# Last MLP of a vision tower: VectorE takes over the rounding of one hidden chunk in six

## The reference, cut to what matters

```
def _L1_ffn_ref(x0, w1, b1, alpha_w1, alpha_a1, w2, b2, alpha_w2, alpha_a2):
    QN, QP = (-8, 7)
    ...
    xq = _quant_act(x0, alpha_a1)                  # round(clip(x / mean(alpha), -8, 7))
    wq1 = _quant_w(w1, alpha_w1)
    x1 = jnp.einsum('bsd,hd->bsh', xq, wq1)
    x1 = x1 * alpha_w1 * alpha_a1.mean() + b1
    x1 = jax.nn.gelu(x1, approximate=False)
    x1 = jnp.clip(x1, -10.0, 10.0)
    hq = _quant_act(x1, alpha_a2)                  # 768 hidden values a token
    wq2 = _quant_w(w2, alpha_w2)
    x2 = jnp.einsum('bsh,dh->bsd', hq, wq2)
    x2 = x2 * alpha_w2 * alpha_a2.mean() + b2
    return x2
h = h + _L1_ffn_ref(_layernorm(h, axis=-1), ...)
```

## Time and profile before

| | |
|---|---|
| median of 3 runs | 2626.57 us (2626.11 to 2627.27) |
| profiled execution, its own time | 2628.79 us |
| its span | 2627.0 us |
| PE busy | 2499.1 us, 95% of the span |
| DVE busy | 2188.3 us, 83% |
| ACT busy | 2098.1 us, 80% |
| POOL busy | 1079.7 us, 41% |

### The profile page before, as it was taken

The page is one execution under the profiler, slowest core; times in us unless marked ns, Lnnn a source line. Parts: engine busy times, 40 slices in busy tenths (PEclk is TensorE's granted clock), DMA queues, the critical chain, the costliest instruction groups (busy, mean ns, idle before and its releaser), DMA issues. The chain is left out here.

```text
span 2627.0 us, 83621 instructions
## 1 busy us (share of the span) xinstructions
PE 2499.1 (95%) x27865; PEld 2135.4 (81%) x27865; DVE 2188.3 (83%) x5770; ACT 2098.1 (80%) x6210; POOL 1079.7 (41%) x1501
## 2 busy tenths in 40 slices
PE   5899999999998999999999999999999999998786
PEld 5788867888787888888888888888888888886565
DVE  5766668888867888888888888888888888887997
ACT  4777767777756888888888888888888888886998
POOL 5677733333322333333333333333333333342233
PEclk9999999999999999999999999999999999999999
DMA  6334410000003333333333333333333333330111
GB/s 179 105 110 119 117 28 9 0 0 36 9 1 71 74 80 69 73 79 71 73 77 72 73 76 73 73 75 75 73 73 76 73 72 78 73 71 11 46 41 51
DMA packets 181843, 173.27 MB, mean 66 GB/s; under 512 B 19206, under 2 KB 180432, under 8 KB 181520
## 3 DMA queue, kind: packets, MB, share of 16 engines
q1 hardware_dynamic: 181776, 172.44, 27.7%
HBM read 46.49 MB, written 9.68 MB: 21 GB/s over the span
## 5 line engine op out<-in xcount | busy, mean ns | idle before, releaser
L1404 POOL TENSOR_TENSOR b_pr<-b_pr,b_rinv 128x394 f32<-128x394 f32 (+1 forms) x768 | 626.1, 842 | 990.6 <-DVE b_rinv L1362 990.6
L1299 ACT ACTIVATE b_pr<-b_banks,b_nmx 128x197 f32<-128x197 f32 (+1 forms) x1536 | 627.8, 424 | 37.4 <-DVE b_nmx L1356 28.9
L1356 DVE TENSOR_REDUCE b_nmx<-b_banks 128x2 f32<-128x394 f32 (+1 forms) x768 | 395.8, 557 | 63.2 <-PE b_banks L1224 59.4
L1208 PE MATMUL b_banks<-b_xt,wqkv 128*128 128x197 f16 x3840 | 383.1, 249 | 3.7 <-DVE b_qk L1346 2.4
L1208 PEld LDWEIGHTS b_banks<-b_xt,wqkv 128*128 128x128 f16 x3840 | 317.0, 98 | 35.2 <-issue 18.9
L1234 PE MATMUL b_bank_t<-ident,b_pr 128*128 128x128 f32 (+3 forms) x3072 | 333.8, 250 | 2.8 <-DVE b_pt L1327 2.7
L1224 PE MATMUL b_banks<-b_kst,b_qst 128*128 128x197 f16 (+1 forms) x3072 | 327.3, 249 | 1.6 <-ACT b_pr L1299 1.6
L1299 ACT ACTIVATION_READ_ACCUMULATOR b_pr<-b_banks,b_nmx 128x1 f32 (+1 forms) x1536 | 314.2, 205 | 0.0
L1234 PEld LDWEIGHTS b_bank_t<-ident,b_pr 128*128 128x128 f32 (+3 forms) x3072 | 287.7, 141 | 22.5 <-issue 8.4
L1224 PEld LDWEIGHTS b_banks<-b_kst,b_qst 128*128 128x128 f16 (+1 forms) x3072 | 265.4, 105 | 20.9 <-issue 11.0
L1346 DVE SCALAR_TENSOR_TENSOR b_qk<-b_banks,b_qk 128x394 f16<-128x394 f32 x384 | 216.3, 563 | 56.7 <-ACT b_qk L1284 56.7
(11 more groups left out here) (244 smaller groups left out, 4904.7 us busy)
## 6 DMA issues: line engine op xcount, KB each, us to landing
b_qst<-b_qk SPq DMA_DIRECT2D x512, 147.8 KB, 2.6
b_kst<-b_qk SPq DMA_DIRECT2D x512, 73.9 KB, 2.3
patches<-in_x SPq DMA_DIRECT2D x64, 588.0 KB, 4.3
out<-z_res SPq DMA_DIRECT2D x32, 192.0 KB
out<-z_res SPq DMA_DIRECT2D x32, 103.5 KB
m_raw_weights<-in_wqkv SPq DMA_DIRECT2D x2, 1152.0 KB, 6.9
m_raw_weights<-in_w SPq DMA_DIRECT2D x2, 576.0 KB, 5.3
h<-in_fc SPq DMA_DIRECT2D x1, 768.0 KB, 5.9
```

Of the source, the lines that this page charges most:

```text
L1208: last = t.matmul(out[:, g * SEQ:(g + 1) * SEQ], w[:, (2 * n + g) * P:(2 * n + g + 1) * P], x, start=(j == 0), stop=(j == 4))
L1299: last = nc.scalar.activation(pr[n % 3][0:ROWS[c], c, e, :], banks[0:ROWS[c], c, e * SEQ:(e + 1) * SEQ], ACT.Exp, bias=nmx[n % 2][0:ROWS[c ...
L1356: v.reduce_max(nmx[n % 2][0:ROWS[c], c, :], banks[0:ROWS[c], c, 0:2 * SEQ].rearrange("p (e t) -> p e t", e=2), AX.X, negate=True).then_inc ...
L1404: last = nc.gpsimd.tensor_tensor(p, p, inv, ALU.mult)
```

## The change

The sixth chunk (f = 5) of each pair is no longer clipped by DVE and then rounded by ACT. DVE does both in a new function `round_last`, in the other order: it first multiplies by 1/alpha and adds the constant, in place, and then limits the sum to bounds that have been moved into the same whole numbers (`limits`, a tile of 128x2 made once at the start of the stage by two small DVE instructions) while writing `z_hid`. The second instruction waits for the first. ACT rounds the other five chunks. The semaphores follow: `hid_done` and `clipped` count five chunks a pair, `last_done` counts the sixth, PE's `down` waits for both, and gelu 3 waits for `last_done` before it writes the tile that the previous pair's sixth chunk held.

```
-                            (clip_hidden(3, 4, 5), 1), (quantise, 3)])
+                            (clip_hidden(3, 4), 1), (round_last, 1), (quantise, 3)])
...
+                for k, bound in enumerate((S["q_lo"], S["q_hi"])):
+                    last = v.tensor_scalar(limits[:, k:k + 1], bound[:], S["inv_a2"][:, 0:1], ROUND + float(LOW_BITS), ALU.mult, ALU.add)
+                last.then_inc(limits_made, 1)
+                dve.wait_ge(limits_made, 1)
...
+                def round_last(u, b):
+                    a = act_out[(2 * b + LAST) % 4][:]
+                    dve.wait_ge(gelu_made, chunks_before(u, b) + HC)
+                    v.tensor_scalar(a, a, S["inv_a2"][:, 0:1], ROUND + float(LOW_BITS), ALU.mult, ALU.add).then_inc(last_scaled, 1)
+                    dve.wait_ge(last_scaled, 2 * u + b + 1)
+                    dve.wait_ge(made_y[b], u)
+                    v.tensor_scalar(hid[b][:, LAST, :], a, limits[:, 1:2], limits[:, 0:1], ALU.min, ALU.max).then_inc(last_done, 1)
...
                 def round_chunk(u, b, f):
-                    n = chunks_before(u, b) + f
-                    act.wait_ge(clipped, n + 1)
+                    if f == LAST:
+                        return
+                    act.wait_ge(clipped, by_scalar(u, b) + f + 1)
...
                         if not first:
-                            act.wait_ge(hid_done, n - 3)
+                            if f == 3:
+                                act.wait_ge(last_done, 2 * u + b)
+                            else:
+                                act.wait_ge(hid_done, by_scalar(u, b) + f - (3 if f > 3 else 2))
...
                 def down(u, b):
-                    pe.wait_ge(hid_done, chunks_before(u, b) + HC)
+                    pe.wait_ge(hid_done, by_scalar(u, b) + LAST)
+                    pe.wait_ge(last_done, 2 * u + b + 1)
```

More of the change, by code:

```diff
@@ L1431, in mlp_1 @@
             two("made_y"), two("scaled"), two("h_done"), two("stored"))
-        fc_made, gelu_made, clipped, hid_done = map(sem, ("z_fc_made", "z_gelu_made", "z_clipped", "z_hid_done"))
+        fc_made, gelu_made, clipped, hid_done, last_scaled, last_done, limits_made = map(sem, (
+            "z_fc_made", "z_gelu_made", "z_clipped", "z_hid_done", "z_last_scaled", "z_last_done", "z_limits_made"))
+        limits = sb("z_limits", [P, 2])
         scaled_rstd = sem("z_scaled_rstd")
@@ L1441, in chunks_before, with by_scalar @@
             return (2 * u + b) * HC
+        LAST = HC - 1
+        def by_scalar(u, b):
+            return (2 * u + b) * LAST
         LAG = 2
```

## The result

The changed kernel takes 2632.28 us (median of 14 runs) against 2626.72 before (14 runs): ratio 1.0024, 95% interval 1.0017 to 1.0031, so slower by 0.24%. The two medians themselves differ by 5.56 us, 0.21%. The forecast was 2632.5.

What follows compares the result with a forecast made beforehand. It took a ring of 13.55 us for two pairs as the bound, then DVE's own line at 6.98 us a step. Middle 5.4 - 0.2, start 0.7, end 0 make +5.9 us, 2626.57 to 2632.5, range 2628.5 to 2638.

Steps and rivals of the forecast that it cites:

- ring of 13.55 us: Last stage, gelus over clip 5, `quantise`, `finish`, `down`, `up` to gelu: 6.78 us a pair, 13.50 for two after.
- DVE's own line: DVE's step in the last stage without waits: 6.50 us before, 6.98 after the change, then the bound.
- 0.28 us of slack: Room DVE has in each step of the last stage, between its line of 6.50 and the step of 6.78.
- the lower bound: New instructions start 0.08 us before clip 4's end, line 6.96; starting 0.04 after it would make 7.08.
- start, to `finish` 0: Start of the last stage: about 0.25 us for two small instructions and 0.46 from `quantise` behind `round_last`, together +0.7.
- 28 steps in the middle: Middle of the last stage: 27 steps from 6.78 to 6.98 us, +5.4, and -0.2 for the low-clock step.
- from `finish` 28 to 31: End of the last stage: last two pairs without `quantise`, ACT gives back what DVE takes, 0, with 0.5 either way.
- -0.2: The middle step at PE's lower clock was expected at some 8.0 us instead of 8.18.
- ACT's waiting: Last stage: ACT's idle time up by about 0.7 us a pair, part of it in front of rounds.
- B: Rival: the two new DVE instructions cost only 0.28 us more than the old one, 2626 to 2628; chance 0.09.
- C: Rival: ACT is the true pacer, each step loses 0.3 to 0.5 us, 2618 or lower; chance 0.05.
- D: Rival: new DVE instructions take 0.55 us each, 2638, or get caught by POOL's additions, 2648; chance 0.12.

Runs made afterwards that it cites:

- e2: Kernel before, plus one extra DVE clip into an unread tile right in front of the clip of chunk 5: 2633.8 us, ratio 1.0037.
- e3: Kernel before, plus one extra DVE clip into an unread tile in front of the clip of chunk 4: 2629.1 us, ratio 1.0010.
- e4: Kernel before, with the clip of chunk 5 moved behind `quantise` in DVE's order, nothing added or left out: 2620.6 us, ratio 0.9978.
- e8: Kernel before, with clip 5 behind `quantise`, clip 1 behind `finish`, and chunk 2 clipped with 3 and 4: 2620.1 us, ratio 0.9978.
- e1: Changed kernel without the second new DVE instruction, so the sixth chunk is never limited: 2619.7 us, ratio to before 0.9973.
- e5: Changed kernel with `round_last` moved behind `quantise` in DVE's order, nothing left out: 2635.3 us, ratio to before 1.0032.
- e9: Changed kernel with `round_last` behind `quantise`, clip 1 behind `finish`, and without POOL's additions of the stream: 2610.8 us, ratio to before 0.9936.
- e6: Changed kernel without POOL's two additions of the stream in each pair: 2625.9 us, ratio to before 0.9999.

## Why the prediction was right

**The ring and the line.** The prediction put a ring of 13.55 us for two pairs and DVE's own line of 6.50 behind the 6.78 us step, with 0.28 us of slack. e2 and e3 confirm both lengths within 0.03 us, e4 opens the ring, and e8's 6.49 agrees with the 6.50, though ACT's own line is 6.49 too and binds there.

**The sum over the step.** DVE's line was forecast at 6.96 to 7.08, with 6.98 taken; it is 6.97. The first new instruction takes 0.412 us on average over its 32 records (0.43 forecast), the second starts 0.45 us behind the first, and the first starts 0.08 us before clip 4's end, not 0.04 behind it: the lower bound was the true one.

**Middle, start and end.** Stage: +5.95 us by the trace, +5.9 forecast. But the parts differ:

| part of the stage | forecast | trace |
|---|---|---|
| start, to `finish` 0 | +0.7 | -0.9 |
| 28 steps in the middle | +5.2 | +6.8 |
| from `finish` 28 to 31 | 0 | 0.0 |

The 28 steps took 2607.16 - 2409.08 = 198.08 us, against 191.26. Two of them, 8.26 and 8.27 us, ran partly at the lower PE clock, where before it was one; each costs 1.3 us over its neighbours. The prediction's -0.2 for such a step (8.0 us instead of 8.18) was wrong in sign. At the start it was the other way: PE's granted clock was 0.76 over 2397 to 2411 us before and 0.88 after, so pair 0's `down` was shorter: from its first group of matmuls to its fourth it took 3.08 us instead of 3.83. What the change itself costs at the start is therefore not shown, beyond the small instructions. The two small instructions cost more than forecast: in front of the first `quantise` 2390.16 - 2389.79 = 0.37 us instead of 0.25.

```profile
2389.79 0.21 DVE L1464 TENSOR_SCALAR z_limits<-q_lo,inv_a 128x1 f32<-128x1 f32 x1
2389.92 0.20 DVE L1464 TENSOR_SCALAR z_limits<-q_hi,inv_a 128x1 f32<-128x1 f32 x1
2390.16 1.25 DVE L1474 TENSOR_SCALAR z_xn<-h,mean,rstd 128x192 f32<-128x192 f32 x4
```

So the total came out to a tenth of a microsecond partly by luck: the clock's stretches cancelled. The difference of the undisturbed steps alone gives 28 x 0.20 = 5.6 us. The medians (+5.6) agree with it, but the interval of the ratio allows 4.5 to 8.1 us, so they can't tell this from the sum with the start in it.

**ACT's waiting.** Forecast was about 0.7 us more a pair, part of it in front of rounds. It is 0.6 (13.7 to 32.6 us and 0.7 over 32 pairs), and nearly all of it stands in front of gelus.

**What the prediction missed.** It measured the path from `finish` over `down`, `up` and the gelus to clip 5 for two pairs, and did not see that the same path leaves it at clip 1 and closes within one. This second ring of 6.61 us lay under both the old mean step and the new one, so it changed nothing here. It is why e1 and e4 gained 0.17 us a step and not 0.29.

**The rivals.** B (the addition is smaller than the slack) fell with 0.45 us measured against 0.28 of slack, and with it the table figure of 0.27 us cited there. C (ACT paces) fell with ACT's 32.6 us of waiting. D (0.55 us an instruction, or POOL in the way) fell with the 0.412 us and with the first new instruction's start, 0.14 us behind the end of POOL's second addition.

## What to carry to other kernels

Before moving an instruction to a less busy engine, work out two lengths for that engine's step: its own line without any waits, with the delays that other engines cause it (here 0.9 us a step from GpSimd), and each ring that passes through it. A move within one ring gives back what it takes, and the slack between ring and line (here 0.28 us) is all that the receiving engine has. Where an ordered queue holds an instruction that waits late (clip 5) in front of one that waits for nothing (`quantise`), swapping them cost nothing and was worth 6 us in the kernel before (e4). In the changed kernel, bound by DVE's own line, the same swap gained nothing (e5), and the moved work, with both its instructions, showed as a gain only with GpSimd's additions gone as well (e9).

## What I had not expected of the hardware

- A wait of DVE for its own instruction at the end of a loop's body cost 0.1 us more than the same wait in the middle of it (e5: 0.51 and 0.41 us start to start), because the loop's branch came behind it; with no such wait at the end there was no such cost (e8).
- A DVE instruction of 128x1 with one scalar operand and a constant took 0.20 to 0.21 us, the one of the same size in the earlier trace rows, with two constants, 0.154.
- In these traces stretches at PE's lower clock level are more frequent in the kernels with the longer steps. Among the 28 steps of the single traces the changed kernel shows two such, e5 three, e2 two, before, e3 and e6 one each, and e1, e4, e8 and e9, the fastest, none. Each step with one was 1.2 to 1.5 us longer than its kernel's mean step. e8 and e9 have one each in their last three steps. These are ten traces, one of each kernel. The mean clocks of all executions bear it out only in part: 0.9949 for e1 and 0.9945 for e4, 0.9936 to 0.9938 for before, 0.9934 for the changed kernel, 0.9928 for e2 and e5, but 0.9930 for e8 and 0.9935 for e9, the two with the shortest steps. So no rule is shown.
